# Third edge stage of a four-layer graph network: the message's scaling on ScalarE, tile by tile

## The reference, cut to what matters

```python
def _mlp(x, ln_w, ln_b, W, b):
    h = _layer_norm(x, ln_w, ln_b)
    h = h @ W.T + b
    return jax.nn.leaky_relu(h, 0.01)
hn = _mlp(node_z, node_ln_w, node_ln_b, node_W, node_b)      # 32 wide
he = _mlp(edge_z, edge_ln_w, edge_ln_b, edge_W, edge_b)      # 32 wide
msg = jnp.concatenate([hn[src], he], axis=-1)                # 64 wide
emb_edge = _mlp(msg, red_ln_w, red_ln_b, red_W, red_b)       # 64 wide
msg_sum = jax.ops.segment_sum(emb_edge, dst, num_segments=n_nodes) + emb_local
deg = jax.ops.segment_sum(jnp.ones((dst.shape[0],), hn.dtype), dst, num_segments=n_nodes)
z = msg_sum / (deg + 1.0)[:, None]
```

## Time and profile before

| | us |
|---|---|
| median of 3 runs | 4975.52 |
| lowest and highest run | 4969.3, 4976.34 |
| the profiled execution | 4972.46 |
| its span, first to last instruction | 4970.7 |
| PE busy | 4058.8 (82%) |
| DVE busy | 4123.6 (83%) |
| ACT busy | 2013.7 (41%) |
| POOL busy | 3249.7 (65%) |

### The profile page before, as it was taken

One profiled execution on the slowest core, in us unless ns is written; L12 is line 12 of the kernel. 1 busy time (PEld: TensorE's weight loads), 2 busy tenths in 40 slices (PEclk: granted clock), 3 DMA queues, 4 the chain that ended last, 5 costly groups with the idle time before them and its releaser, 6 DMA issues. The chain is left out here.

```text
span 4970.7 us, 104763 instructions
## 1 busy us (share of the span) xinstructions
PE 4058.8 (82%) x29353; PEld 2725.1 (55%) x29528; DVE 4123.6 (83%) x7954; ACT 2013.7 (41%) x6556; POOL 3249.7 (65%) x2950
## 2 busy tenths in 40 slices
PE   4999999999688888757777777588888887299998
PEld 2555555554344444435555655355555554299998
DVE  6888888888788888758888888688888887899997
ACT  3777676777111111135445544111111110377774
POOL 5777777774477777636666666377777776155554
PEclk6999999999788988869999999799999998599998
DMA  4444444442122222112222222255555554111111
GB/s 137 108 101 106 105 102 105 102 102 70 43 52 50 51 51 51 40 36 54 55 51 55 55 53 49 66 137 133 133 136 132 147 133 107 35 48 48 48 48 32
DMA packets 493105, 394.00 MB, mean 79 GB/s; under 512 B 346007, under 2 KB 379168, under 8 KB 492904
## 3 DMA queue, kind: packets, MB, share of 16 engines
q1 hardware_dynamic: 395496, 303.53, 21.6%
q0 software_dynamic: 90560, 83.37, 10.3%
q10 hardware_dynamic: 6976, 6.23, 0.4%
HBM read 355.34 MB, written 37.42 MB: 79 GB/s over the span
## 5 line engine op out<-in xcount | busy, mean ns | idle before, releaser
L1093 POOL DMA_INDIRECT edge_src_rows<-table_wh,edge_gather_idx x806 | 852.7, 1058 | 332.0 <-issue 254.8
L950 POOL DMA_INDIRECT edge3a_src_rows<-table_h,edge3a_gather_idx x808 | 763.7, 945 | 312.7 <-issue 241.2
L1123 PE MATMUL edge_sums_ps<-edge_onehot_src,edge_halves 128*128 128x512 bf16 (+1 forms) x4689 | 857.0, 327 | 22.1 <-DVE edge_onehot_src L1211 13.6
L950 POOL DMA_INDIRECT table_cat<-table_hn,table_gather_idx x592 | 616.1, 1041 | 303.8 <-issue 158.8
L1508 POOL DMA_INDIRECT edge_src_rows<-table_h,edge_gather_idx x608 | 611.8, 1006 | 285.7 <-issue 170.1
L1123 PEld LDWEIGHTS edge_sums_ps<-edge_onehot_src,edge_halves 128*128 128x128 f16 x4840 | 383.6, 97 | 430.1 <-DVE edge_halves L1301 8.3
L2170 PE MATMUL edge3a_z_ps<-Wz,edge3a_both_ends_t 128*128 128x396 f32 x1616 | 585.7, 513 | 9.9 <-DVE edge3a_terms L2263 8.2
L2582 PE MATMUL edge3b_sums_ps<-edge3b_onehot,edge3b_weighted 128*128 128x128 f32 x4848 | 571.4, 278 | 7.1 <-DVE layers_accT L2620 5.2
L2499 POOL TENSOR_TENSOR edge3b_weighted<-edge3b_src_rows,edge3b_alpha 128x1920 f32<-128x1920 f32 x101 | 350.3, 3469 | 344.5 <-DVE edge3b_alpha L2599 250.6
L2582 PEld LDWEIGHTS edge3b_sums_ps<-edge3b_onehot,edge3b_weighted 128*128 128x128 f32 x4848 | 552.2, 193 | 12.8 <-DVE layers_accT L2620 5.4
L2263 DVE SCALAR_TENSOR_TENSOR edge3a_terms<-edge3a_z_ps,att_z 128x792 f32<-128x792 f32 x404 | 391.2, 976 | 155.1 <-PE edge3a_z_ps L2170 154.6
(11 more groups left out here) (370 smaller groups left out, 7685.4 us busy)
## 6 DMA issues: line engine op xcount, KB each, us to landing
edge_dst_row<-in_dst_row SPq DMA_DIRECT2D x102, 512.0 KB
edge3a_dst_row<-in_dst_row SPq DMA_DIRECT2D x102, 512.0 KB
edge_window<-table_wh_parts SPq DMA_DIRECT2D x816, 48.8 KB
edge3a_window<-table_h SPq DMA_DIRECT2D x816, 32.0 KB
edge_edge_attr<-in_ea SPq DMA_DIRECT2D x101, 256.0 KB
kept_rows<-edge3a_src_rows SPq DMA_DIRECT2D x101, 256.0 KB
edge3b_src_rows<-kept_rows SPq DMA_DIRECT2D x101, 256.0 KB
edge_edge_attr<-in_ea SPq DMA_DIRECT2D x101, 128.0 KB
```

Of the source, the lines that this page charges most:

```text
L950: nc.gpsimd.indirect_dma_start(self.slot(b, j), None, self.table[:, :], bass.IndirectOffsetOnAxis(ap=self.idx[b][:, j:j + 1], axis=0)).the ...
L1093: nc.gpsimd.indirect_dma_start(g[q][:, j, :], None, k.t_wh[:, :], bass.IndirectOffsetOnAxis(ap=idx[q][:, j:j + 1], axis=0)).then_inc(gathe ...
L1123: mm = pe.matmul(acc[:, i, 0:w], halves[q][:, j, a, :, :].rearrange("p h d -> p (h d)"), hot[:, o:o + w], start=first and a == 0, stop=False)
```

## The change

ScalarE multiplies the message by one over the root, tile by tile, with the reciprocal as a per-row scale of a copy: eight instructions a batch in place of VectorE's one. They stand behind ScalarE's copy of the following batch's turned rows and ahead of that batch's two roots. VectorE keeps the reciprocal, the shift and the leaky relu.

```diff
+                def scale(n):
+                    act.wait_ge(inv2, n)
+                    wait_past(act, u_b, n - 1)
+                    for j in range(B):
+                        a = act.activation(u[:, j, :], rp[:, j, 0:D], ACT.Copy, scale=st[:, 5, j:j + 1])
+                    a.then_inc(u_sc, 1)
+
                 def body(t, first, last):
...
                         act.wait_ge(catTp_ready, n + 2)
                         act.activation(catT[:, :, :], catTp[:, :, :], ACT.Copy).then_inc(catT_ready, 1)
+                        if not (first and h == 0):
+                            scale(n - 1)
                         if not empty(last, h + 1):
...
                 ends_apart(act, body)
+                scale(USED)
...
-                def scale(n):
+                def invert(n):
                     dve.wait_ge(std2_ready, n)
                     dve.reciprocal(st[:, 5, :], st[:, 4, :]).then_inc(inv2, 1)
-                    dve.wait_ge(inv2, n)
-                    dve.tensor_tensor(u[:, :, :], rp[:, :, 0:D], over(st[:, 5, :], D),
-                                      ALU.mult).then_inc(u_sc, 1)
...
                         if not (first and h == 0):
-                            scale(n - 1)
+                            invert(n - 1)
...
-                scale(USED)
+                invert(USED)
```

## The result

The changed kernel takes 4993.59 us in the median of 7 runs, beside 4975.52 for the kernel before: a ratio of 1.0042, 95% interval 1.0032 to 1.0052. It is slower by 18 us in the medians and by 21 in the ratio, where 20 us less were forecast. The profiled execution took 4995.54 us.

What follows compares the result with a forecast made beforehand. VectorE was taken to bound first, second and third, ScalarE's chain the taken batch. +1.25 - 0.90 - 0.97 - 0.20 = -0.82 us a group, x 25 = -20 us, from 4975.5 to 4955 us; range 4939 to 4990.

Steps and rivals of the forecast that it cites:

- The register load hides: On VectorE's queue, the 0.6 us load starts before the reciprocal, so the add follows directly: 0.97 us freed a batch.
- four places: The four batches of a steady group in the third edge stage; together forecast to change by -0.82 us a group.
- second: Batch b = 1 of a group: VectorE keeps its pace, -0.97 us, from 8.38 to 7.41.
- first: Batch b = 0 of a group: VectorE keeps its pace, -0.90 us, from 8.83 to 7.93.
- open-load rival: VectorE's load between reciprocal and add stays exposed; VectorE gains only 0.22 us a batch, +17 us in all; chance 0.10.
- taken batch: Batch b = 3 of a group: starts 0.30 us earlier, ScalarE's chain 1.55 longer, so +1.25, to 13.79 us.
- ScalarE's step: Each of eight added ScalarE instructions a batch costs 0.105 + 0.089 = 0.194 us, together 1.55 us.
- dearer step: Rival: each added ScalarE instruction costs 0.240 us, the chain is 0.37 us longer, -3 us in all; chance 0.17.
- third: Batch b = 2 of a group: ScalarE becomes the bound, -0.20 us, from 6.95 to 6.75.
- The step that failed: In first and second VectorE keeps its pace, -0.90 and -0.97 us, as ScalarE's chain ends earlier, about 6.75 us in.
- clock rival: TensorE's low clock over `sum_up` in second delays ScalarE's chain to 8.41 us; +4 us, up to +16; chance 0.18.
- GpSimd and SyncE: Gathers and edge attribute loads: no DMA moves, GpSimd has 2.9 us slack a group; both costed at nothing.

Runs made afterwards that it cites:

- e1: Changed kernel plus idle TensorE products, while it waits for the scaled message and after the message product of first and second; 4953.70 us, ratio 0.9965.
- e8: Changed kernel with idle TensorE products only where TensorE waits for the scaled message; 4964.96 us, ratio 0.9983.
- e9: Changed kernel with idle TensorE products only behind the message product of first (6) and second (5); 4952.05 us, ratio 0.9961.
- e4: Changed kernel, but ScalarE scales only in the taken batch and VectorE keeps the product in the other three; 4987.71 us, ratio 1.0037.
- e5: Changed kernel, but VectorE keeps the product in the taken batch, plus idle TensorE products; 4919.61 us, ratio 0.9896.
- e7: Kernel before, with the window starts read ahead of the message's reciprocal in every batch; 4940.96 us, ratio 0.9938.

## Why the prediction was wrong

*What held, by steps.* The register load hides in three of the four places: the add follows the reciprocal at once in second, and first and second gain 0.86 and 1.11 us where the clock is whole (e1), not the 0.22 of the open-load rival, which is out. In the taken batch a gap of 0.46 us marked "issue" stays (2732.31). ScalarE's step was taken as 0.194 us and is 1.58 / 8 = 0.197; the dearer step is out. The Trainium skill's ACTIVATE figure ("ScalarE: Activation LUTs", What ACT_TABLE_LOAD costs), from which the prediction worked out an estimate of 239 ns for 64 columns, is too high for this input in PSUM, where 0.197 us was measured. First was forecast at 7.93 and is 7.91; third 6.75 and 6.78. Taken was forecast at 13.79 and is 13.74 in 12 of 24 groups; in e1, where the clock is whole, the four places are 13.81, 7.97, 7.27 and 6.82, together 35.87, against 35.88 forecast. That the sum agrees to 0.01 is luck: second is 0.14 shorter than forecast, and the others are longer by 0.02 to 0.07. e1's ratio of 0.9965 is 17 us less than before: the forecast of -20 was that of the kernel with a steady clock.

*The step that failed* is the one on first and second, with its condition "This needs `sum_up` in second to run fast", and the sentence in the clock rival that was to secure it: the gap shrinks "to about 2.2 us, shorter than the gap that was harmless". In the changed kernel `sum_up` ran slow behind a gap of 1.62 us, where 2.36 had been harmless before, and in e8 the same gap of 2.21 us stands before a fast one and a slow one. One gap and its successor were taken for a rule; they were not. The length of the single gap ahead of a product did not decide.

*The rival on TensorE's clock named the mechanism and priced half of it.* It put second at 8.41 us in place of 7.41, which would have turned -20 into +4, or +16 with a longer low clock. Second came out at 8.26, 25 x 0.85 = 21 us over the forecast: that price was about right, and by itself it would have made the time the same as before. What neither the forecast nor a rival prices is the other half: the low clock also falls on the message product and `choose` at the end of third. TensorE now waits for ScalarE ahead of the message product in every batch (1.47 us at 2688.99) and runs short of work through the whole group; with idle products in these waits (e8) or behind the message products of first and second (e9) `choose` is fast again. Against the batch at 2728.36, the late `choose` holds the first `take` of the one at 2690.85 back by 1.24 us and its first add by 1.60; the batch lasts 15.36 in half the groups, so 25 x 0.75 = 19 us in the mean. 21 + 19 = 40 turn -20 into the stage's +20.

*GpSimd and SyncE* were rightly put at nothing. GpSimd still waits for the message product (3.3 us in a group, 2.9 before), and no TensorE wait in the groups shown is for a gather.

*Left open*: what exactly makes the clock fall. e1, e8 and e9 show where idle products prevent it, not the rule, and not why only half the groups have it over `choose`.

## What to carry to other kernels

When work moves to another engine, look not only at whether that engine has time, but at who will now stand and wait for it: here four TensorE waits a group, 6.5 us together and at most 2.42, brought the low clock to a place where it costs. A low clock that costs nothing is a price already standing in the profile; before cover is removed from it, ask in which products it will fall next, and price them all at half speed, or test the steady case with idle products. And move an operation only in the rounds in which its old engine is the bound: the same edit cost 18 us in one batch of four (e4) and, once the clock was held, gained in the other three (e5).

## What was not expected of the hardware

The clock was low over products behind a gap of 1.62 us here and whole behind one of 2.36 in the kernel before, and in e8 it was both behind gaps of 2.21. Adding 11 idle products a group in two places (e9) left it low only where that costs next to nothing, 21 in four other places (e8) left it low over second in some groups, 26 (e5) or 32 (e1) kept it whole. A register load of 0.6 us, placed behind a wait for the engine's own previous result, cost 0.32 us each time; put ahead of that wait in the kernel before it gave 31 us (e7), more than the 17 us that the change itself gives at a steady clock (e1).
